# A float32 decoder layer on one core: new order in the opening, at the seam of its two stages and in the last tiles

## What is computed

```python
x = x + L0_attn(ln(x))    # 16 heads of 128, qkv = silu(x Wqkv), blocks of 64 with decay exp(-s*distance)
                          # out = norm_w * o * rsqrt(mean(o*o)+eps); (sigmoid(x Wg) * out) Wout
x = x + L0_xattn(ln(x))   # softmax(x ctx^T / sqrt(512)), masked, times ctx
x = x + L0_ffn(ln(x))     # rows scaled by max|.|/448 and rounded; gate, up (1408 wide), silu(g)*u,
                          # scaled and rounded again, down
```

## Time and profile before

| | us |
|---|---|
| median of 3 runs | 2632.61 (2632.53 to 2634.94) |
| the profiled execution | 2630.53 |
| its span, first to last instruction | 2628.8 |

### The profile page before, as it was taken

How to read it: one execution, slowest core, us unless ns; L and a number is a source line. 1 busy time by engine, 2 the same in 40 slices (tenths; PEclk the granted TensorE clock), 3 DMA queues, 4 the chain that set the end, 5 groups by cost and what they waited for, 6 DMA issues and landing times.

```text
span 2628.8 us, 37692 instructions
## 1 busy us (share of the span) xinstructions
PE 2577.9 (98%) x12735; PEld 2102.3 (80%) x12735; DVE 2130.2 (81%) x4130; ACT 1100.7 (42%) x1862; POOL 690.5 (26%) x1030
## 2 busy tenths in 40 slices
PE   9999999999999999999999999999989999999995
PEld 7888888888888888888888888888877676767762
DVE  8888888887778888777888888777747888888887
ACT  4433333433335444333534443343324555555553
POOL 2111211311122231111223211022223444444444
PEclk9999999999999999999999999999999999999998
DMA  5555455444347654444665544363566555556632
GB/s 217 215 209 189 146 187 192 159 141 129 133 154 235 187 162 160 133 143 139 197 209 187 165 144 129 136 249 144 192 224 181 159 156 167 152 162 168 164 109 56
DMA packets 244943, 439.05 MB, mean 167 GB/s; under 512 B 100240, under 2 KB 135952, under 8 KB 236048
## 3 DMA queue, kind: packets, MB, share of 16 engines
q1 hardware_dynamic: 161056, 407.90, 46.1%
q10 hardware_dynamic: 81360, 20.07, 4.3%
q0 software_dynamic: 2336, 8.65, 1.6%
HBM read 286.35 MB, written 130.17 MB: 158 GB/s over the span
## 4 chain that ended last, share of the span: by engine, by line
PE 93%; DVE 4%; DMA 2%; issue 1%; ACT 1%; POOL 0%; SPq 0%; ACTq 0%; DVEq 0%; POOLq 0%
PE bank L834 39%; PE bank L1529 13%; PE bank L815 13%; PE bank L950 9%; PE bank L904 9%; PE bank L1573 6%; PE bank L1583 3%; PE bank L1550 1%; DMA attention_shared<-attention_x_in 1%; PE bank L1539 1%; DVE attention_stats L1007 0%; DMA finish_qT<-finish_q 0%; PE bank L842 0%; DMA finish_tT<-down_named 0%; PE bank L1561 0%
## 5 line engine op out<-in xcount | busy, mean ns | idle before, releaser
L834 PE MATMUL bank<-attention_xT,attention_w_hi 128*128 128x512 f32 x3064 | 948.4, 391 | 0.0
L834 PEld LDWEIGHTS bank<-attention_xT,attention_w_hi 128*128 128x128 f32 x3064 | 571.3, 188 | 114.5
L834 PE MATMUL bank<-attention_xT,attention_w_lo 128*128 128x512 f32 x1532 | 597.2, 390 | 0.0
L608 POOL TENSOR_TENSOR attention_sq_sum<-attention_sq_sum,attention_sq 128x512 f32<-128x512 f32 x120 | 188.3, 1569 | 966.9 <-ACT attention_sq L777 966.9
L834 PEld LDWEIGHTS bank<-attention_xT,attention_w_lo 128*128 128x128 f32 x1532 | 287.9, 188 | 59.6
L815 PE MATMUL bank<-attention_w_hi,attention_xT 128*128 128x512 f32 x1024 | 325.9, 400 | 9.6 <-DVE attention_sig_v L984 9.4
L734 ACT CAST attention_sh<-attention_sf 128x384 fp32r<-128x384 f32 (+1 forms) x384 | 186.0, 548 | 283.9 <-DVE attention_sf L1133 283.8
L1529 PE MATMUL bank<-finish_w_out_hi,finish_og 128*128 128x512 f32 x824 | 282.8, 408 | 0.2
L1143 DVE TENSOR_TENSOR attention_sl<-attention_sf,attention_sh 128x384 fp32r<-128x384 f32 (+1 forms) x384 | 227.8, 649 | 0.0
L815 PEld LDWEIGHTS bank<-attention_w_hi,attention_xT 128*128 128x128 f32 x1024 | 184.5, 190 | 42.9 <-issue 11.0
L1175 DVE SCALAR_TENSOR_TENSOR attention_og<-bank,attention_nw,attention_gate 128x512 f32<-128x512 f32 x128 | 96.0, 750 | 132.6 <-PE bank L950 119.1
(11 more groups left out here) (225 smaller groups left out, 4921.7 us busy)
## 6 DMA issues: line engine op xcount, KB each, us to landing
attention_xT<-normed_turned SPq DMA_DIRECT2D x62, 2048.0 KB, 8.6
gated_heads<-attention_og_out SPq DMA_DIRECT2D x64, 1024.0 KB, 7.7
finish_og<-gated_heads SPq DMA_DIRECT2D x103, 512.0 KB, 3.9
values<-attention_held SPq DMA_DIRECT2D x128, 256.0 KB, 2.8
attention_vh<-values SPq DMA_DIRECT2D x32, 512.0 KB, 8.1
attention_vl<-values SPq DMA_DIRECT2D x32, 512.0 KB, 9.4
finish_og_last<-gated_heads SPq DMA_DIRECT2D x25, 512.0 KB, 4.0
normed_turned<-attention_shared SPq DMA_DIRECT2D x24, 512.0 KB, 4.1
```

Source lines behind the costliest of these rows:

```text
L608: g.tensor_tensor(sq_sum[:, col_b], sq_sum[:, col_b], sq[:, :], ALU.add).then_inc(s_acc, 1)
L834: mm = pe.matmul(dst[:, :], part[a][w][:, k, col:col + P], xT[i][:, b, k, :], start=(k == 0 and s == 0), stop=(k == KD - 1 and s == 2))
```

## The change

What it does, place by place.

- Opening: DVE's order becomes queries 0, statistics of tile 1 rows 0 and 1, values 0, statistics 2, keys 0, values 1, statistics 3.
- Odd slots: the second values (PE, ACT, DVE) move behind the query and key rows of that slot.
- Seam: the last two eighths of `w_out_lo` go from POOL to DVE (`w_out_rest`), `sum_squares` goes ahead by one quarter of a projection, `root_of_squares` goes ahead of `masks` and `mem_lo_of`, which move into step -2; on SP the loads of x tiles 4 to 7 move behind the ring's ninth load, the wait for the last store behind the sixth, and the down weights to step 0.
- Last tiles: the step loop stops before tile 31's own step, and the tails are written out. Tile 31 (`L`) has its own buffers, its maximum is taken in two pieces and its turn in two pieces of 6 and 5 blocks; `down` of tiles 29, 30, 31 has a bank each; all four last `y_scaled` stand at the end of DVE, with the addition to x on DVE too; PE fills three gaps with `keep_warm` (45, 16 and 130 small matmuls).
- Some semaphores are merged (`s_rs2` into `s_nb`, `s_max` into `s_soft`), `sy` has four columns.

```diff
@@ attention, gpsimd and scalar
-            if n == LAST - 1:
-                w_out_lo(6)
-            if n == LAST:
-                w_out_lo(PARTS - 1)
-            if q is not None:
+            if q is not None and j == 0:
                 sig_values(q + 1)
...
                 sig_query(n + 1)
                 sig_key(n + 1)
+            if q is not None and j == 1:
+                sig_values(q + 1)
@@ attention, tensor
-            if begun_in(n - 1) is not None:
+            if begun_in(n - 1) is not None and j == 0:
                 values(begun_in(n - 1) + 1)
...
                 head_rows(K_BANK, w, P, i2).then_inc(s_k, 1)
+            if begun_in(n - 1) is not None and j == 1:
+                values(begun_in(n - 1) + 1)
@@ attention, vector
         queries(0)
-        all_stats_of(1)
+        first_stats_of(1, (0, 1))
+        values(0)
+        first_stats_of(1, (2,))
         keys(0)
-        values(0)
         values(1)
+        first_stats_of(1, (3,))
...
-            if q is not None:
+            if q is not None and j == 0:
                 values(q + 1)
             if not end:
                 queries(n + 1)
                 keys(n + 1)
+            if q is not None and j == 1:
+                values(q + 1)
+    def w_out_rest(v):
+        v.wait_ge(s_wlo, 6)
+        for q in range(6, PARTS):
+            part_ = slice(q * CH, (q + 1) * CH)
+            v.wait_ge(s_whi, q + 1)
+            v.tensor_tensor(early.wo[1][:, part_, :], raw_out[:, part_, :], early.wo[0][:, part_, :].bitcast(F32),
+                            ALU.subtract).then_inc(s_wlo, 1)
@@ finish, sync
-        early.wait_stored(sp, B - 2)
-        for m in range(4, SLOTS):
-            early.load_x(sp, m)
-        early.wait_stored(sp, B - 1)
...
                 if (n, q) == (-3, 0):
+                    early.wait_stored(sp, B - 1)
                     load_weights("u", upT, s_uT)
+                if (n, q) == (-3, 3):
+                    for m in range(4, SLOTS):
+                        early.load_x(sp, m)
-                if (n, q) == (-1, 2):
+                if (n, q) == (0, 2):
                     sp.wait_ge(early.s_sum, B)
                     load_weights("d", downT, s_dT)
@@ finish, gpsimd: behind the loop, which now ends before L
+        silu_up(K, 1)
+        silu_up(K, 2)
+        rstd3(L)
+        for i in range(NF):
+            silu_up(L, i)
@@ finish, scalar: behind the loop
+        t_turned(J)
+        t_magnitude(K)
+        silu(L, 0)
+        silu(L, 1)
+        silu(L, 2)
+        t_scaled(K)
+        last_scaled()
+        t_turned(K)
+        last_turned(0)
+        last_turned(1)
@@ finish, tensor
             if tile(n + 3):
                 project(n + 3, 1)
+            if n + 3 == 0:
+                early.sum_squares(pe)
...
-            if n + 3 == 0:
-                early.sum_squares(pe)
...
+        gate_up(K, 2)
+        down(I)
+        pe.wait_ge(s_x2, T)
+        keep_warm(45)
+        gate_up(L, 0)
+        gate_up(L, 1)
+        keep_warm(16)
+        gate_up(L, 2)
+        down(J)
+        keep_warm(130)
+        down(K)
+        last_down()
@@ finish, vector
+        early.w_out_rest(v)
         attention_over(v)
-        masks()
-        mem_lo_of(0, 0)
-        mem_lo_of(0, 1)
         early.root_of_squares(v)
...
+            if n + 2 == 0:
+                masks()
+                mem_lo_of(0, 0)
+                mem_lo_of(0, 1)
...
+        x_round_sum(L)
+        x_round_out(L)
+        scaled_gate_up(K, 2)
+        t_round_sum(J)
+        t_round_out(J)
+        t_scale(K)
+        gate_up_scale(L)
+        for i in range(NF):
+            scaled_gate_up(L, i)
+        last_scale()
+        t_round_sum(K)
+        t_round_out(K)
+        last_round(0)
+        last_round(1)
+        for m in range(I, T):
+            y_scaled(m)
```

More of the change, by code:

```diff
@@ L1023, in all_stats_of, with first_stats_of @@
                 stats_of(m, t)
+        def first_stats_of(m, tiles):
+            v_.wait_ge(*landed(m))
+            for t in tiles:
+                stats_of(m, t)
         def shifted(m, t):
@@ L1277, in finish, with t_of, down_bank @@
     s_tT, s_d, s_yo = sem("t_turned"), sem("down_summed"), sem("y_scaled")
+    s_tl = [sem(f"last_t_turned{i}") for i in range(2)]
+    PIECES = ((0, 6), (6, KF))
+    I, J, K, L = range(T - 4, T)
     PASSES = [(0, 0), (0, 1), (1, 0)]
     STEPS = range(-3, T + 3)
+    def t_of(m):
+        return t_last if m == L else t_
+    def down_bank(m):
+        return {J: Y_BANK, K: T_BANK, L: X_BANK}.get(m, D_BANK)
     def tile(m):
@@ L1403, in gpsimd @@
         g.wait_ge(s_k, 4)
-        for n in range(-2, T + 3):
+        for n in range(-2, L):
             if tile(n):
@@ L1490, in scalar @@
         mem_hi_of(0, 1)
-        for n in range(-2, T + 2):
+        for n in range(-2, L):
             if tile(n + 1):
@@ L1578, in down @@
             pe.wait_ge(s_tT, 16 * m + 16)
-            after(pe, s_yo, m)
+            if m == J:
+                pe.wait_ge(s_x1, T)
+            elif m == K:
+                pe.wait_ge(s_hTc, T)
+            else:
+                after(pe, s_yo, m)
             if m == 0:
@@ L1582, in down, with last_down, keep_warm @@
             for k in range(KF):
[L1583 removed]
+                mm = pe.matmul(down_bank(m)[:, :], tT[:, k, :], downT[:, :, k, :], start=(k == 0), stop=(k == KF - 1))
             mm.then_inc(s_d, 1)
[L1586 removed]
+        def last_down():
+            for i, (a, e) in enumerate(PIECES):
+                pe.wait_ge(s_tl[i], 16)
+                for k in range(a, e):
+                    mm = pe.matmul(X_BANK[:, :], tT_last[:, k, :], downT[:, :, k, :], start=(k == 0),
+                                   stop=(k == KF - 1))
+            mm.then_inc(s_d, 1)
+        def keep_warm(times):
+            for _ in range(times):
+                pe.matmul(X_BANK[:, 0:P], c.ident_bf[:, :], c.ident_bf[:, :], start=True, stop=True,
+                          skip_group_check=True)
+        for n in range(-3, L):
             if tile(n + 1):
```

90 lines of the change are left out of this document (61 added, 29 removed).

## The result

The changed kernel took 2618.82 us in the median of five runs (2615.73 to 2623.89), the kernel before 2634.94 beside it: ratio 0.9945, 95% interval 0.9934 to 0.9956, 16.1 us faster. Forecast were 2604 and a gain of 28.75 us; 2618.8 lies above the range of 2597 to 2616. The profiled execution has a span of 2617.4 us against 2628.8.

What follows compares the result with a forecast made beforehand. TensorE (PE) was taken to bound the kernel, 93% of the chain, so only less idle or a better clock helps. 3.9 + 5.9 + 11.95 + 7.0 = 28.75 us off 2630.53, plus 2.1 for the median: 2604, range 2597 to 2616.

Steps and rivals of the forecast that it cites:

- Opening: Start of the kernel: values 3 start 2.2 us earlier and a low clock worth 1.7 us goes; 3.9 us together.
- Odd slots: Attention's odd slots: moving values saves 4.7 us of waits and 1.7 of low clock, less 0.5 charged; 5.9 us.
- Seam: From the last slot's O into tile 1: shorter waits, earlier root, full clock and reordered loads; 11.95 us.
- Rival D: Opening and odd slots only shift their waits and the tail gives its lower bound: gain 19 us, 2614; chance 0.12.
- C: Rival: moved values hit the odd slots, late products make PE wait at slot ends: 34 us, 2638; chance 0.02.
- my bound of 3 us for the new waits: Odd slots: upper bound on new waits caused by the moved values, charged at 0.5 us, lower bound 0.
- Root and addition: Seam, before tile 1: the root finishes early, hidden by PE's quarters; the 8.10 us wait shrinks by 7.15.
- rival A: Seam: its wait becomes one for ring buffers; up to 6 us come back, 2610; chance 0.12.
- My cover of 2.5 us for the ring: Seam: 7.8 MB of loads at 399 GB/s take 19.5 us plus 2 latency, in time by 2.5 us.
- step a: Seam, last slot's O: POOL's w_out_lo piece, blamed for DVE's slow subtraction and late cast, leaves; 1.3 us gained.
- step b: Seam: DVE does both output-weight pieces at the end, 2.5 us (bounds 2.5 and 6), before PE wants them.
- Tail: Last tiles: tile 31's maximum ends 4.35 us earlier, split turn 1.35, full-clock last down 1.3; 7.0 us, bounds 2 and 9.

Runs made afterwards that it cites:

- odd_old_order: The changed kernel with the odd slots back in the order of before on PE, ACT and DVE: 2611.64 us, ratio 0.9917.
- load_first_late: The changed kernel, but from slot 94 on SP issues the next turned input's load ahead of the second values' store in odd slots: 2610.96 us.
- late_load: odd_old_order with SP waiting, in odd slots with new values, for the slot's O before issuing the turned input's load: 2623.05 us.
- narrow_passes: The changed kernel with DVE's three passes over down-projection weight rows covering 512 of 1408 columns, the rest left unrounded: 2610.20 us.
- load_first: The changed kernel with SP issuing the next turned input's load ahead of the second values' store in all odd slots: 2615.01 us.
- odd_until_94: The changed kernel with the new odd-slot order only before slot 94 and the order of before from there: 2614.16 us.
- rows_first: The changed kernel with DVE's passes over the weight rows put ahead of the next queries and keys in odd slots: 2615.40 us.
- masks_ahead: odd_old_order with masks and the first memory halves back ahead of the root on DVE at the seam: 2619.04 us.
- fillers_none: odd_old_order without the 45, 16 and 130 filling matmuls: 2611.34 us.
- fillers_more: odd_old_order with 76 and 147 filling matmuls in place of 45 and 130: 2609.46 us.
- loads_as_before: odd_old_order with SP's order of the loads at the seam as before: 2614.91 us.

## Why the prediction was wrong

**The failed step is "Odd slots"**, forecast at 5.9 us faster; in the profiled execution it is 8.65 slower, 7 by the medians of odd_old_order. Without it the sum was near: 22.85 us forecast, 22.95 by the medians of odd_old_order (2634.59 less 2611.64) and 20.1 by the milestones of the profiled execution. That the first agrees to 0.1 is luck: its interval is about 3.5 us to either side, and opening, seam and tail each came out short. Within the step two sentences failed.

- "SP waits for the second store's data later too; behind it stand only the next turned input (wanted after the gates) and the slot's own stores." I named the queue and costed it at nothing, because I asked only when the load is wanted, not what it meets when it starts later. It put the load 3.9 us behind the gates; the gated store and the turned weight rows landed late, DVE stood still for 9.6 us and ACT for 14, PE behind them: 7.7 us, 9.3 with the low clock in slot 98 (load_first_late, late_load).
- "Next in line is the value tile at the end of the slot": next in line was also the gated output, with it the first product of the following slot. I placed the product at 11.4 in a slot of 15 without the two passes of 1.62 us that DVE still owes ahead of the gated output in slots 97 and 103. 2.8 us (narrow_passes beside load_first_late). Of the 0.4 us that I gave slot 97, 0.29 us came there, and 2.27 in slot 98. The gap that the product left, 2.33 us of DVE in slot 97, was where it cost least.

The gains came: slots 1 and 97 give 5.0 us in the ruler. But slot 2, where statistics stand ahead of the gated output, lost 2.75, and in load_first_late, where S is taken away, slots 1, 2 and 97 to 105 add up to +0.85 us. Nor is all of it the order's: of the 3.8 us in slot 97, 1.6 are the low clock that I booked as 1.7. In eleven kernels with the old order there, the kernel before among them, the wait of 2.0 us stays, and only three have the low clock behind it. Taken together the new order in the odd slots earned about nothing even without S, as load_first_late (2610.96) beside odd_old_order (2611.64) says too. Rival D named the shift of slot 2's wait; C had the place right (moved values hit the odd slots) and the mechanism half. Its price of 34 us is what comes off the forecast, and 14.5 came off (5.9 and 8.65). Both had small chances, and my bound of 3 us for the new waits cut off what happened.

- **Opening**: 3.1 to 3.8 us at slot 0 in the ruler of every kernel that has it, 3.9 forecast. One wait of 1.37 stays, about 1.5 forecast; the clock in 36 to 40 us is 1.00, not 0.57:

```profile
36.00:40.00 4.00, 4.00 (x20) 3.30 (x18) 3.97 (x6) 4.00 (x8) 3.82 (x4) 1.00 0.12 41
```

- **Seam**: 10.7 of 11.95. Root and addition gave 7.1 of 7.15 (idle 1.00 us before tile 1's projection); the root ended at 1950.9, not before 1946, 4.0 us of it because the seam came later, and stayed hidden. The full clock behind it gave 1.8 of 2.0, `qT` 2.1 instead of 1.5. A wait of 0.73 for a ring buffer, a small piece of rival A, and what stands around it took 0.9 back, and another 0.7 went in the last two tiles before PE's loop end. My cover of 2.5 us for the ring was worked out with 399 GB/s; it came out as that wait of 0.7 us. By the 358 GB/s of the Trainium skill (DMA: Bandwidth & Descriptors, "Where 436 GB/s comes from") the wait would have been longer; the trace moved 393 and 397 GB/s in 1954 to 1962 and disagrees again.
  In step a the gain came, 1.35, but I had read the rows wrongly: DVE's subtraction of 1.75 us at 1930.40 did not run beside `w_out_lo`, which had ended at 1930.09, but beside POOL's next addition, which started 0.08 us ahead of it. `w_out_lo` had held up only the cast, by 0.3 us, and so let the addition go first, as far as POOL's rough spans can be read. In the changed kernel the subtraction goes first, and the addition is the longer one:

```profile
1930.32 1.29 POOL L608 TENSOR_TENSOR attention_sq_sum<-attention_sq_sum,attention_sq 128x512 f32<-128x512 f32 x1 [0.23 <-ACT attention_sq L777]
```

```profile
1935.46 0.69 DVE L1193 TENSOR_TENSOR attention_og_out<-attention_og,attention_og_out 128x512 fp32r<-128x512 f32 x1
...
1935.67 1.63 POOL L606 TENSOR_TENSOR attention_sq_sum<-attention_sq_sum,attention_sq 128x512 f32<-128x512 f32 x1 [11.28 <-ACT attention_sq L775]
```

  The two pieces of step b on DVE took 3.45 us instead of 2.5 and stayed hidden; they start 0.4 us into such an addition (1942.99, 1.62 us), which fits the single wait for it that I named beside the sum.
- **Tail**: 6.1 of 7.0. The maximum of tile 31 ended 19.1 us behind PE's loop end, 18.9 forecast. The fillers run at 0.057 us, not the 0.070 that I took from the 160 at the start. That mean mixes two rates, as windows of the kernel before would have shown (the count stands behind PE's busy time):

```profile
1.00:4.00 3.00, 2.92 (x28) 2.93 (x29) 0.93 (x2) 1.28 (x1) 1.97 (x11) 1.00 0.45 79
...
8.00:12.00 4.00, 4.00 (x75) 4.00 (x73) 3.48 (x18) 1.00 (x3) 0.00 (x0) 1.00 1.05 401
```

  28 take 3 us, later 75 take 4. So the 130 fall 0.97 us short of tile 30's turn; `qT` lands 2.3 us after the 45. `down` of tile 31 takes 2.54 us, as forecast, but two `down`s follow each other now, and only the first would have run slow.

## What to carry to other kernels

When a step is moved later in one engine's program, its stores move with it, and everything that stands behind them in the DMA-issuing queue moves too. Here the order of two entries in one queue was worth 8 us. Ask of each of those transfers what it will collide with, not only when its data is wanted. And before moving an operation out of the way of another, look whether it sits in a gap of its engine: what comes behind it in the new place (here 3.2 us of passes and the output that frees the next product) is what it will delay.

## What the runs showed of the hardware

- One and the same store of the gated output (1024 KB, slot 97) took 5.8, 11.0 or about 20 us to land, by what was in the queues: the load of 2048 KB issued 8.4 us, 4.9 or 4.5 ahead of it, with the weight rows' DMA transpose issued between them. The transpose itself landed after 3.9, 13.2 and 21.8 us. The distance alone does not explain it: in narrow_passes the load went out only 2.6 us ahead and the store landed after 12.0, and at one and the same distance of 4.9 us it landed after 10.8 in odd_old_order and 15.8 in odd_until_94. Which overlap stretches the store so far stays open.
- The clock does not follow a wait by a fixed rule. After 2.41 us of idle in slot 2 PE's granted clock was 0.62 in the changed kernel, a mix of 1.2 and 2.4 GHz, and after 2.42 us in rows_first it stayed at 1.00. Behind the 2.0 us of slot 97 it stayed full in eight of the eleven kernels that have this wait. Slot 2, first the changed kernel, then rows_first:

```profile
74.00:78.00 4.00, 3.38 (x9) 2.72 (x10) 3.93 (x8) 0.41 (x1) 1.80 (x4) 0.62 0.75 199
```

```profile
74.00:78.00 4.00, 3.75 (x17) 3.13 (x18) 3.93 (x9) 0.75 (x2) 1.54 (x3) 1.00 0.82 197
```

- With the same code up to the seam, odd_old_order, masks_ahead, fillers_none, fillers_more and loads_as_before were 0.97, 1.74, 5.24, 3.53 and 2.82 us ahead at slot 126. One profiled execution is good for where time goes, but not for steps of 2 us in a sum; the 9.3 of S and 8.65 of the step have to be taken with that, and rest on the medians beside them.
